# Mamba-style layer with a mixture-of-experts FFN on one core: a first sequence with split loads and three late weight folds, and a joint in another order

## The reference

```python
x = x + attn(layernorm(x))            # per sequence
#   proj = rmsnorm(h) @ w_in_proj     -> z 256, x 256, B 512, C 512, dt_raw 8
#   x  = silu(causal conv of 4 taps(x) + conv_b)
#   dt = softplus(dt_raw @ w_dt + b_dt), mean over 32 channels of each of 8 heads
#   y  = chunked scan over (x, dt, B, C), + x*D, * silu(z); rmsnorm; @ w_out_proj
x = x + ffn(layernorm(x))
#   shared: 2 experts 128->512->128 with relu, mean of both
#   routed: 4 experts 128->512->128, the best two of a softmax gate, weighted
```

## Time and profile before

| | us |
|---|---|
| median of 3 runs (588.93, 589.76, 590.2) | 589.76 |
| the profiled execution | 591.66 |
| its span on the core | 589.9 |
| mean granted TensorE clock in it | 0.986 |
| busy: PE / DVE / ACT / POOL | 552.3 / 449.1 / 355.3 / 177.6 |

### The profile page before, as it was taken

The page is one execution under the profiler, slowest core; times in us unless marked ns, Lnnn a source line. Parts: engine busy times, 40 slices in busy tenths (PEclk is TensorE's granted clock), DMA queues, the critical chain, the costliest instruction groups (busy, mean ns, idle before and its releaser), DMA issues.

```text
span 589.9 us, 11815 instructions
## 1 busy us (share of the span) xinstructions
PE 552.3 (94%) x3992; PEld 431.1 (73%) x3992; DVE 449.1 (76%) x1050; ACT 355.3 (60%) x761; POOL 177.6 (30%) x232
## 2 busy tenths in 40 slices
PE   6897789999999999999999999999999999999995
PEld 5675667777787777777777777777777777877783
DVE  4789766978689776997679777898778777675654
ACT  3784378737685387735786376744786376752341
POOL 2067102530145211532145302452136202352010
PEclk8998989999999999999999999999999999999998
DMA  6451005400371005600163005500074004600120
GB/s 205 123 147 53 0 1 165 131 2 1 93 176 47 2 1 153 162 1 0 49 187 74 0 0 151 160 0 0 11 206 95 0 1 125 160 11 1 38 57 18
DMA packets 36921, 41.41 MB, mean 70 GB/s; under 512 B 3307, under 2 KB 27285, under 8 KB 36885
## 3 DMA queue, kind: packets, MB, share of 16 engines
q1 hardware_dynamic: 36240, 40.78, 25.5%
q10 hardware_dynamic: 644, 0.17, 0.2%
HBM read 37.79 MB, written 3.15 MB: 69 GB/s over the span
## 4 chain that ended last, share of the span: by engine, by line
PE 40%; DVE 15%; issue 15%; POOL 10%; ACT 6%; DMA 1%; DVEq 0%; POOLq 0%; ACTq 0%; SPq 0%
PE bank L417 8%; PE bank L419 6%; PE bank L418 6%; PE bank L635 4%; PE bank L637 4%; PE bank L636 4%; DVE cv L1105 3%; DVE act_l L1251 3%; POOL seg L1462 3%; POOL CTe L1448 3%; ACT act_h L860 3%; PE bank L528 2%; DVE late L1259 2%; POOL late L1471 2%; POOL xw L1458 1%
## 5 line engine op out<-in xcount | busy, mean ns | idle before, releaser
L1251 DVE SCALAR_TENSOR_TENSOR act_l<-bank,act_h 128x512 fp32r<-128x512 f32 x192 | 131.4, 687 | 81.9 <-ACT act_h L860 80.6
L860 ACT ACTIVATE act_h<-bank 128x512 fp32r<-128x512 f32 x192 | 114.5, 596 | 96.8 <-PE bank L419 92.8
L1471 POOL TENSOR_TENSOR late<-late 128x512 f32<-128x512 f32 x31 | 45.2, 1458 | 221.5 <-DVE late L1259 221.5
L417 PE MATMUL bank<-fTl,w1h 128*128 128x512 f32 x192 | 86.3, 450 | 4.2 <-DVE act_l L1251 4.2
L635 PE MATMUL bank<-act_l,w2h 128*128 128x512 f32 x192 | 78.5, 409 | 4.1 <-DVE late L1259 2.3
L880 ACT ACTIVATE seg<-seg,lneg 128x128 f32<-128x128 f32 x256 | 81.3, 392 | 0.9 <-DMA seg<-lc_rows 0.8
L418 PE MATMUL bank<-fTh,w1l 128*128 128x512 f32 x192 | 75.8, 395 | 0.0
L419 PE MATMUL bank<-fTh,w1h 128*128 128x512 f32 x192 | 75.6, 394 | 0.0
L637 PE MATMUL bank<-act_h,w2h 128*128 128x512 f32 x192 | 75.5, 393 | 0.0
L636 PE MATMUL bank<-act_h,w2l 128*128 128x512 f32 x192 | 75.3, 392 | 0.0
L1458 POOL TENSOR_TENSOR xw<-xs,seg 128x128 f32<-128x128 f32 x48 | 19.7, 410 | 138.3 <-ACT seg L880 71.5
(11 more groups left out here) (176 smaller groups left out, 1073.1 us busy)
## 6 DMA issues: line engine op xcount, KB each, us to landing
seg<-lc_rows SPq DMA_DIRECT2D x32, 512.0 KB, 4.3
late<-gk_rows SPq DMA_DIRECT2D x8, 1024.0 KB, 9.2
grow<-lc_rows SPq DMA_DIRECT2D x48, 128.0 KB, 5.3
x_in<-L_attn_hidden_dram SPq DMA_DIRECT2D x8, 256.0 KB, 2.8
out_dram<-late SPq DMA_DIRECT2D x8, 256.0 KB, 2.4
late<-L_ffn_sw_dram SPq DMA_DIRECT2D x2, 512.0 KB, 6.0
late<-L_ffn_rw_dram SPq DMA_DIRECT2D x1, 1024.0 KB, 6.6
CT<-L_attn_w_in_proj_dram SPq DMA_DIRECT2D x1, 772.0 KB, 6.8
```

The costliest lines, as they stand in the source:

```text
L417: mm(dst, stat_h, mov_l, start=True, stop=False)
L860: nc.scalar.activation(act_h[:, b % RING, :], HID[b % 2][:], ACT.Relu).then_inc(act_h_ready, 1)
L1251: v_.scalar_tensor_tensor(act_l[:, r, :], HID[b % 2][:], 0.0, f(act_h[:, r, :]), ALU.max, ALU.subtract)\
L1471: g.tensor_tensor(acc, acc, term, ALU.add).then_inc(acc_ready, 1)
```

## The change

1. **Loads.** w_in_proj comes in four DMAs with a semaphore each: x columns, z columns and B/C columns from SP, the eight dt columns from ACT (line 1536 to 1544 of its columns). The six row vectors and conv_w move from ACT's queue to SP's, behind those loads.
2. **Weights.** Folds 3, 4 and 5 move from the opening into steps 0 to 2 of body 1, in the place of 12 keep_busy matmuls. ACT makes the high part of W1 (`w1_high`), DVE only the difference (`w1_low`). POOL takes the W2 differences of experts 2 to 5 in body 1, once the norm of sequence 0 is applied, and no longer in the opening. `keep_busy_early` gets 8 more matmuls ahead of the transposes of hn, 5 in place of 3 behind them, and 4 in each of chunks 2 and 3.
3. **Joint.** `act_low` of older's block 20 stands between statistics and aggregation; `dt_add` stands ahead of the convolution, whose taps are spread over steps 2 and 3; on ACT `silu_x(s, 1)` stands behind the first two copies of B.
4. **Terms.** `routed_out` stands ahead of `act_low` at steps 5, 17 and 21; the first `add_term` stands behind POOL's chunk 2 (step 18, not 17).
5. **Tail.** `out_transposes` and `store` of sequence 6 at step 9, not 7; the last two `second` of body(None, 7, 6) are interleaved with the `first` of body(None, None, 7).

```diff
 # SP
-            sp_eng.dma_start(w_raw, a["w_in_proj"]).then_inc(win_in, 16)
+            for lo, hi, landed in ((256, 512, wx_in), (0, 256, wz_in), (512, 1536, wbc_w_in)):
+                sp_eng.dma_start(w_raw[:, lo:hi], a["w_in_proj"][:, lo:hi]).then_inc(landed, 16)
...
+                sp_eng.dma_start(rows[r:r + v.shape[0], :], v).then_inc(rows_in, 16)
 # PE, body
-                    if is_seq(s, 1) and i in (0, 1, 3):
-                        keep_busy(FOUT, 4)
+                    if is_seq(s, 1) and i < 3:
+                        fold_weights(i + 3)
+                        fold_bias(i + 3)
...
-                    if older is not None and i == 7:
+                    if older is not None and i == (7 if s is not None or prev is None else 9):
                         out_transposes(prev, older)
...
+                    if prev is None and i < LAG:
+                        second(older, NBLK - LATE - LAG + i)
-                if prev is not None:
+                if prev is not None and s is not None:
                     second(prev, NBLK - LATE - 2)
                     second(prev, NBLK - LATE - 1)
 # PE, opening
+                keep_busy_early(8)
                 hn_transposes(0)
...
-                keep_busy_early(3)
+                keep_busy_early(5)
...
-                    fold_weights((1, 3, 4, 5)[c])
+                    if c < 2:
+                        fold_weights(c + 1)
+                        fold_bias(c + 1)
+                    else:
+                        keep_busy_early(4)
 # ACT
+            def w1_high(g):
+                act.wait_ge(fold_psum, g + 1)
+                nc.scalar.copy(w1h[:, g, :], HID[g % 2][:]).then_inc(w1h_set, 1)
...
-                if i in (3, 4):
-                    silu_z(s, i - 3)
-                    silu_x(s, i - 3)
+                if i == 3:
+                    silu_z(s, 0)
+                    silu_x(s, 0)
                 if i == 4:
+                    silu_z(s, 1)
                     b_copy(s, 0)
                     b_copy(s, 1)
+                    silu_x(s, 1)
...
+                    if is_seq(s, 1) and i < 3:
+                        w1_high(i + 3)
...
-                chunk_decays(0)
                 b_copy(0, 2)
                 b_copy(0, 3)
+                chunk_decays(0)
 # DVE
-                v_.memset(carrier[:, RING:RING + 1], 0.0)
+                if older is not None:
+                    act_low(older, NBLK - LATE)
+                else:
+                    v_.memset(carrier[:, RING:RING + 1], 0.0)
...
+                    if older is not None and i == 3 + LAG:
+                        routed_out(older, 3)
...
+                    if prev is not None and i in (15 + LAG, 19 + LAG):
+                        routed_out(prev, (i - 15 - LAG) // 4)
+                    if (new := block_at(i, prev, older)) and not (i == 0 and prev is not None):
                         act_low(*new)
+                    if is_seq(s, 1) and i == 0:
+                        w1_low(3)
...
                         if i == 1:
-                            conv(s, 1, range(TAPS))
-                        if i == 2:
                             dt_add(s, 0)
                             dt_add(s, 1)
+                        if i == 2:
+                            conv(s, 1, (0, 1))
                         if i == 3:
+                            conv(s, 1, (2, 3))
                             dt_clamp(s)
 # POOL
-                    if step == 2 and c < NCH - 1:
-                        w2_low(2 * c)
-                        w2_low(2 * c + 1)
+                    if step == 2 and c < 2:
+                        w2_low(c)
...
+                if is_seq(s, 1):
+                    pool.wait_ge(fn_ready, NCH)
+                    for n in range(2, NG):
+                        w2_low(n)
...
-                    if prev is not None and i in (15 + LAG, 19 + LAG):
+                    if prev is not None and i in (16 + LAG, 19 + LAG):
                         add_term(prev, (i - 15 - LAG) // 4)
```

More of the change, by code:

```diff
@@ L324, in _ @@
             sp_eng.dma_start(x_in[:], x_dram[0]).then_inc(x_loaded, 16)
-            sp_eng.dma_start(wn_in[:], a["w_norm_in"].rearrange("(p b) -> p b", b=1)).then_inc(wn_in_in, 16)
-            sp_eng.dma_start(w_raw, a["w_in_proj"]).then_inc(win_in, 16)
+            for lo, hi, landed in ((256, 512, wx_in), (0, 256, wz_in), (512, 1536, wbc_w_in)):
+                sp_eng.dma_start(w_raw[:, lo:hi], a["w_in_proj"][:, lo:hi]).then_inc(landed, 16)
+            src = [a["sb1"].rearrange("n (b p) -> (n b) p", p=P), a["rb1"].rearrange("n (b p) -> (n b) p", p=P),
+                   a["sb2"], a["rb2"], a["conv_b"].rearrange("(b p) -> b p", p=P), a["w_norm_out"].rearrange("(b p) -> b p", p=P)]
+            r = 0
+            for v in src:
+                sp_eng.dma_start(rows[r:r + v.shape[0], :], v).then_inc(rows_in, 16)
+                r += v.shape[0]
+            sp_eng.dma_start(conv_w[:], a["conv_w"].rearrange("(b p) one k -> p b (one k)", p=P)).then_inc(conv_in, 16)
             sp_eng.dma_start(gb[:], a["gate_b"].partition_broadcast(P)).then_inc(small_in, 16)
@@ L632, in second @@
                 pe.wait_ge(act_l_ready, nth(prev, NBLK, b + 1))
-                if is_seq(prev, 0) and b == 0:
-                    pe.wait_ge(w2l_set, NG)
+                if is_seq(prev, 0) and k == 0:
+                    pe.wait_ge(w2l_set, g + 1)
                 mm(dst[:], w2h[:, g, k, :], act_l[:, r, :], start=begins, stop=False)
@@ L938, in body @@
                         scan_part(s, i)
-                    if prev is not None and i == 9:
+                    if is_seq(s, 1) and i < 3:
+                        w1_high(i + 3)
+                    if prev is not None and i == (9 if s is not None else 11):
                         keep_x1(prev, older)
@@ L967, in opening @@
             def opening():
-                src = [a["sb1"].rearrange("n (b p) -> (n b) p", p=P), a["rb1"].rearrange("n (b p) -> (n b) p", p=P),
-                       a["sb2"], a["rb2"], a["conv_b"].rearrange("(b p) -> b p", p=P), a["w_norm_out"].rearrange("(b p) -> b p", p=P)]
+                act.dma_start(wn_in[:], a["w_norm_in"].rearrange("(p b) -> p b", b=1)).then_inc(wn_in_in, 16)
+                act.dma_start(w_raw[:, 1536:1544], a["w_in_proj"][:, 1536:1544]).then_inc(wcol_in, 16)
                 act.dma_start(w_dt[:], a["w_dt"]).then_inc(wdt_in, 16)
                 act.dma_start(b_dt[:], a["b_dt"].partition_broadcast(P)).then_inc(bdt_in, 16)
-                r = 0
-                for v in src:
-                    act.dma_start(rows[r:r + v.shape[0], :], v).then_inc(rows_in, 16)
-                    r += v.shape[0]
-                act.dma_start(conv_w[:], a["conv_w"].rearrange("(b p) one k -> p b (one k)", p=P)).then_inc(conv_in, 16)
                 act.dma_start(a_log[:], a["A_log"].partition_broadcast(P)).then_inc(alog_in, 16)
@@ L1011, in opening @@
                     c_copy(0, b)
+                w1_high(0)
                 decays(0, 0, 0)
@@ L1181, in add_residual, with norm2 @@
                         .then_inc(x1_ready, 1)
-            def norm2(prev):
+            def norm2(prev, older):
                 dve.wait_ge(x1_ready, nth(prev, 4, 4))
@@ L1299, in body @@
                             add_residual(prev)
-                            norm2(prev)
+                            norm2(prev, older)
                         if i == 5:
@@ L1327, in body @@
                                 conv(s + 1, 0, (2, 3))
-                    if older is not None and i == 3 + LAG:
-                        routed_out(older, 3)
-                        if is_seq(older, n_seq - 1):
-                            last_term(older)
-                    if prev is not None and i in (15 + LAG, 19 + LAG):
-                        routed_out(prev, (i - 15 - LAG) // 4)
-                if prev is not None:
+                    if older is not None and is_seq(older, n_seq - 1) and i == 1:
+                        routed_out(older, 2)
+                if prev is not None and s is not None:
                     routed_out(prev, 2)
@@ L1371, in opening @@
                     c, step = divmod(i - CHUNKS_FROM, 3)
-                    if step == 0:
-                        for n in ((0,), (1,), (2, 3), (4,))[c]:
-                            w1_parts(n)
+                    if step == 0 and c < 3:
+                        w1_low(c)
                     scan_part(0, i)
@@ L1476, in body @@
                     rsqrt2(prev)
-                if older is not None and not is_seq(older, n_seq - 1):
-                    add_term(older, 3)
+                if is_seq(s, 1):
+                    pool.wait_ge(fn_ready, NCH)
+                    for n in range(2, NG):
+                        w2_low(n)
+                if older is not None:
+                    add_term(older, 2 if is_seq(older, n_seq - 1) else 3)
                 for i in range(CHUNKS_FROM, NBLK):
```

30 lines of the change are left out of this document (14 added, 16 removed).

## The result

| | us |
|---|---|
| before, median of 4 runs (588.93, 589.76, 590.2, 590.82) | 589.98 |
| changed kernel, median of 4 runs (574.92, 575.16, 576.64, 577.49) | 575.9 |
| ratio, with its 95% interval | 0.9765 (0.9735 to 0.9795) |
| changed kernel on another occasion: median; ratio | 576.66; 0.9787 (0.9748 to 0.9826) |
| its profiled execution; span; clock | 576.64; 574.9; 0.996 |

It is faster by 14.1 us, 2.3%. The forecast was 573.0, with 567 to 581 as range.

A forecast was written before the change was run, and what follows sets the result against it. Steady bodies were taken as PE-bound except some 2 us of standstills each; the opening as late work, then half clock. 3.2 + 4.5 - 0.3 + 6.6 + 2.8 = 16.8 us off gave 573.0 against the median, range 567 to 581.

The forecast's parts named there:

- rival 1: Joint: ACT takes it all, last tap 0.45 us later than walked, proj(11) not earlier; 4 us lost, 577; chance 0.20.
- Opening, 7.7: Opening: gain of 3.2 us in its first part and 4.5 us in its second.
- the first part: Opening up to ACT's copy of x: earlier dt and x columns, eight extra matmuls, clock at full level; 3.2 us gained.
- The low stretch: Opening, second part: half of the 1.7 us cost of a stretch of 3.3 us at half clock was taken off.
- Body 1, 0.3 lost: Body 1: three folds and differences added, one tap meeting POOL's differences; 0.3 us lost, ends 1.5 lost and 0.7 won.
- Bodies 2 to 7, 6.6: Six steady bodies: 1.1 us gained each, 6.6 in all; ends 0.5 and 1.5 each.
- 0.45 for the joint: Each steady body: what remains of 1.5 us from block 20 and dt_add after fTl and ACT are late.
- 0.65 for the two waits at steps 17 and 20: Each steady body: 0.4 us from routed_out ahead of act_low, 0.25 from POOL's first add behind masks and CTe.
- the joint's list of what is late next: Steady joint: after block 20 and dt_add, fTl is late, then ACT's chain from last tap to B3 before proj(11).
- Tail, 2.8: Tail: waits at out_transposes and between first and second go, as does block 20's; 2.8 us gained, ends 1.5 and 3.5.
- the price of 0.75: Tail: act_low behind routed_out makes `first` two blocks on wait 0.25 us, three times; 0.75 lost.
- rival 2: Opening: clock stays low, eight new matmuls take 0.43 us each, first part gives 0; 578; chance 0.15.

The follow-up runs named there:

- relu_first: The changed kernel with relu of block 0 ahead of silu_x(s, 1) on the scalar engine at step 4; 574.29 us, ratio 0.9739.
- joint_undone: The changed kernel with only the joint of the bodies back in its old order; opening, terms and tail stay changed; 587.23 us, ratio 0.9942.
- after_again: The changed kernel itself, unedited, measured and profiled once more on another occasion; 576.66 us, ratio 0.9787.

## Why the prediction was right, and where not

The time lay in the range and in the forecast's own one of 570 to 576.5. By the number alone rival 1 (577) was nearer, but its signs, bodies of 67.0 and a long wait for B, are absent. The changed kernel's profiled execution was forecast at 574.9 and was 576.64.

- **Opening, 7.7: 7.2** (7.5 by the mean of seven). The copy of x came 3.0 earlier, against the 3.1 to 3.5 walked, and y_product of chunk 3 8.9 (60.20 to 51.27; the prediction had "some 8"), of which the squares keep 8.16. The reasons given for the first part were wrong, though: neither the split of w_in_proj (0.4) nor the eight matmuls carry it. With both undone 2.46 of the 3.0 stay, and 6.25 of the 7.2. That the number came out is luck there. I had costed two edits by one row before and never asked what the re-ordered queue alone would do. The low stretch that the sum half allowed for came, in 54.9 to 58.3, at 1.2 us. Two terms of the walk were off: the eight matmuls took 1.9 us (7.95 to 9.84) and not 1.7, and hn of chunk 2 took 2.63 and not 1.3.
- **Body 1, 0.3 lost: 0.25 lost.** One tap met POOL, as taken: 1.67 less 0.75 is 0.92. What the prediction did not see is that this rests on the new joint: by the old one all three taps meet it, 5 us.
- **Bodies 2 to 7, 6.6: 5.4**, and 6.4 by the mean of seven profiles. The walk along the chains held to 0.1 us at three places. Its parts did not: 0.45 for the joint and 0.65 for the two waits at steps 17 and 20 are no separate gains. The step that failed is the joint's list of what is late next. It ends at B3 and leaves out step 5, where relu behind the later softplus holds act_low, and act_low would hold routed_out. The move of that term, which I costed at nothing, is worth 0.8 a body, and without the moves of the terms the joint loses 0.4 a body. Rival 1 (ACT takes the whole joint) did not come, but relu_first shows how near it is.
- **Tail, 2.8: 2.6.** Both waits went, and the price of 0.75 was 0.7.
- **From the sum to the median.** The execution of before that was profiled lay 1.7 us above the median of before; the one of the changed kernel lay 0.7 above its own. I had let the full 1.9 carry over. With the sum's 1.8 that makes the 2.9 us between 573.0 and 575.9.

The Trainium skill ("SBUF — State Buffer", section "SBUF: two separate sides") calls the port pair of VectorE and GpSimd an exclusive lock that a VectorE instruction with two SBUF inputs takes as a whole, against a GpSimd instruction that reads SBUF. The taps have two such inputs, and in the changed kernel one took 1.67 us in place of 0.75, while w1l, with one input in PSUM, kept its 0.68 beside the same POOL work. joint_undone bears the lock out instruction by instruction; here are its three taps and two of the four differences:

```profile
65.75 1.66 DVE L1119 SCALAR_TENSOR_TENSOR cv<-xpad,conv_w,cv 128x512 f32<-128x512 f32 x1
66.81 1.73 POOL L1410 TENSOR_TENSOR w2l<-late,w2h 128x512 fp32r<-128x512 f32 x1
67.44 1.65 DVE L1119 SCALAR_TENSOR_TENSOR cv<-xpad,conv_w,cv 128x512 f32<-128x512 f32 x1
68.51 1.71 POOL L1410 TENSOR_TENSOR w2l<-late,w2h 128x512 fp32r<-128x512 f32 x1
69.13 1.63 DVE L1119 SCALAR_TENSOR_TENSOR cv<-xpad,conv_w,cv 128x512 f32<-128x512 f32 x1
```

They end in turn, at 67.41, 68.54, 69.09, 70.22 and 70.76: each difference 1.13 us behind a tap, each tap 0.55 behind a difference. So a pair takes 1.68 us, which is less than the 2.02 that their rows add up to undisturbed (0.75 and 1.27): a row also holds time in which the other engine can work. What a meeting costs is better taken from such ends than from the sum of two rows, or from the lengths of rows that contain the waiting.

## What to carry to other kernels

Two moves in one joint can need each other: ask for every moved instruction what stands behind it in its engine's list and holds a buffer, and try each half alone, for one of the halves may be a loss. An instruction that frees a buffer goes ahead of one that waits for another engine. Where work is moved beside another engine's, look at which of its instructions the neighbour will meet, not at the sum of both, and hold it back with a wait if they clash.

## What was not expected of the hardware

- The first instruction of the convolution has one tensor input and is slowed too, but not always. Beside POOL's differences it took 1.14 us in joint_undone, 0.83 to 0.87 in six other profiles and 0.54, its time alone, in three, the changed kernel's among them. In joint_undone the difference in progress ended 0.85 us behind its start, in after_again (0.87) 0.59, and in the changed kernel 0.18 (66.48 plus 1.31, less 67.61).
- At least one stretch at half clock, of 3.3 us or more, stands in the opening of every profile, but its place changes from execution to execution: two with one code had it at 54.9 (changed) and near 47.5 (after_again). The first came behind a wait of PE of 2.22 us, the second behind three waits of 0.70 to 0.77, which the first had as well, without a fall. The opening varied by 1.8 us over seven profiles of the same code.
- The ten matmuls at the very start take 4.64 us (from 2.14), the eight like them at 7.95 take 1.9. The profile shows a granted clock of 1.00 for both. The price of 0.43 each that rival 2 put on the new ones did not come; why the first ten are so slow stays open.
